# Asking for the tokens of a tile ahead of its first weights, with four buffers late in the expert loop of a fused transformer layer

## The chip, the cores and the metric

The kernel runs on one core of one Trainium2 chip. The metric is device time in microseconds (us) for one launch of the whole layer. TensorE (PE) does matrix products and transposes, VectorE (DVE) and ScalarE (ACT) the elementwise work, GpSimd (POOL) indirect transfers and some elementwise work, and SyncE (SP) issues plain DMA transfers. Each engine runs its own list of instructions in order. They meet only at semaphores: an instruction that waits holds up all that stands behind it on its engine.

## What is computed

```python
x = x + attn(layernorm(x))                # efficient attention, one head of 256
x = x + xattn(layernorm(x), ctx)          # causal cross attention, 16 heads of 64
y = layernorm(x)                          # 4096 tokens of 256
probs = softmax(y @ router_w + router_b)  # 16 experts
topw, topi = top_k(probs, 4); topw /= sum(topw)
for e in range(16):                       # each token counts for its 4 experts only
    x += (gelu(y @ w1[e] + b1[e]) @ w2[e] + b2[e]) * gate[:, e]
```

x is 8 batches (B) of 512 tokens by 256, w1 is 16 x 256 x 512, w2 is 16 x 512 x 256, all fp32. Every product is made of three products in a reduced fp32 form, from a high and a low part of each side (`split3`): a "split" of a matrix is one copy that rounds to the high part and one subtraction that gives the low part.

## The kernel before

Three stages follow each other: the first attention, the cross attention with the routing of each batch, and the expert tiles. The change lies in the last, and in the few microseconds where the second goes over into it.

**One list for all engines.** `attention_plan()` writes a list of (step, index) by hand. Each engine walks that one list and emits its own part of each step (the functions `tensor`, `scalar`, `vector`, `gpsimd`, `sync`), so the order of the list is the order of every engine's queue.

**Routing.** The rows of each batch, with their gates and token numbers, are scattered by POOL into `rows_dram`, sorted by expert (steps `scatter`, and `scatter_last` for the last batch). Rows that fill up an expert's last tile are written by SP (step `pad`, two experts in each of the iterations 9 to 16, two transfers per expert).

**Expert tiles.** 79 tiles (`MOE_TILES`) of 256 rows of one expert each. Which expert and which row a tile starts at is read from tables, for the first 24 tiles (`SURE_TILES`) from a table made before the last two batches were routed. The steps of tile j are:
- `load_x` (SP): 256 rows of 273 floats into `x_in[j % 2]`. It waits until tile j - 2 has been turned (`t_pe`) and its gates copied out (`tail_set`).
- `load_w1` (SP): the 512 KB of its expert's w1 into `w1_raw[j % 2]` (the tiles `ahead.ctx32` and `ahead.x1_0`, free by then). It waits until tile j - 2's w1 has been split (`w1_hi`, `w1_lo`).
- `turn_x`: four transposes (PE) into one bank, the high part by ACT, the low part (`x_lo`) and the copy of the gates (`tail`) by DVE.
- `split_w1` (DVE): the two parts of w1, and the tile's b1.
- `hidden`: 24 matmuls (PE), GELU and high part (ACT), low part (DVE).
- `results`: 24 matmuls with w2 (PE), scaling by the gate into `y` (ACT), and two indirect transfers that add the rows to `out` (POOL). POOL first waits until the adds of the one or two tiles before have landed, where these may touch the same tokens (at a change of expert), and ACT waits for the add of tile j - 3.

Iteration j of the loop holds, in this order: load x of j+2, turn x of j+1, hidden of j, split w1 of j+2, load w1 of j+4, results of j-1. The routing steps of the last batch (`CHAIN`) are strewn over the iterations 1 to 10. Up to tile 11 (`CHAIN_END`) all tiles use one bank for `turn_x`, since the other belongs to these steps.

**Between the stages** the 16 matrices of w2 are split (`high_w2` by ACT, `low_w2` by DVE, or by POOL for those in `LOW_BY_POOL`). The last seven of them stand around `turn_x` 0 and `output` of the last batch; `results` of any tile waits for all.

Of the kernel before, what the change touches and what calls it, by code (L numbers as in the profile page):

```python
# [930 lines left out]
def attention_plan():  # L931
    plan = [("begin", None), ("project_k", 0), ("project_v", (0, 0)), ("project_q", 0), ("project_v", (0, 1))]
    split_w2 = lambda *mine: [(step, e_) for step in ("high_w2", "low_w2") for e_ in mine]
    for n in range(B * PAIRS + 1):
# [60 lines left out]
def cross_attention(nc, sems, spent, d, x1_dram, x1_stored, out, rows_dram, routing, W, projecting, ahead, kept, hold, plan):  # L995

    with ExitStack() as stack:
# [118 lines left out]
        def sync(sp, w, step, at):  # L1116
# [7 lines left out]
            elif step == "add_b2" and at[1] == 1:  # L1124
                b = at[0]
                w.wait_ge(b2_ev, at)
# [511 lines left out]

def experts(nc, sems, d, rows_dram, out, routing, held, ahead, kept, gone):

    with ExitStack() as stack:
# [334 lines left out]
```

## Time and profile before

| | |
|---|---|
| time, median of 3 runs | 1805.8 us (1803.61 to 1812.94) |
| the profiled execution's own time | 1795.01 us |
| its span, first to last instruction | 1793.3 us |
| mean granted TensorE clock | 0.972 of full speed |
| busy: PE, DVE, ACT, POOL | 91%, 67%, 60%, 28% |

The span is cut below at starts of `turn_x`, the first step of a tile on PE. Each stretch then holds a whole number of tiles: tiles 0 to 3, 4 to 11, 12 to 19, 20 to 76, and the last two with the end. In the views `ex_X` is the bank of `turn_x`, `kept_x` is `x_in`, `ahead_ctx` and `ahead_x` are `w1_raw`, `ex_w` the split w1, `ex_H` and `ex_Y` the banks of `hidden` and `results`, `expert_rows<-ahead_spare` a `pad`, and `experts_w_hi`, `experts_w_lo` the two parts of w2. The granted clock is either full (2.4 GHz) or half (1.2 GHz); a mean between them says how the stretch was divided.

### The profile page before, as it was taken

What the parts mean: (1) busy time and instruction counts of PE and PEld (TensorE: products, weight loads), DVE (VectorE), ACT (ScalarE), POOL (GpSimd) and SP (SyncE); (2) the same over time, 40 slices, a digit from 0 to 9 for tenths busy, and PEclk for the clock granted to TensorE, in tenths of its full rate; (3) what the DMA queues carried; (4) which work ended last, traced back from release to release, by engine and by line L of the source; (5) the groups of instructions that cost most, each with busy time, mean ns of one, the idle gap of its engine ahead of it and who ended that gap; (6) DMA issues with size and microseconds to landing.
All of it is one profiled execution on the core that took longest, in us unless ns stands there. A gap on an engine that the chain in (4) does not pass through costs nothing.

```text
span 1793.3 us, 35763 instructions
## 1 busy us (share of the span) xinstructions
PE 1623.1 (91%) x12470; PEld 1360.6 (76%) x12470; DVE 1195.2 (67%) x2752; ACT 1078.5 (60%) x2702; POOL 505.0 (28%) x432
## 2 busy tenths in 40 slices
PE   5899889999999999999999999878778989888886
PEld 4788767777776777777777777578778888888886
DVE  6988756677677776777677766876445555555552
ACT  4555466766666666766676666856345555655553
POOL 2444300000302103012030130344544444443444
PEclk9999989999999999999999999989889999999998
DMA  3121110000201101001010021645766666665663
GB/s 93 36 83 71 46 50 1 1 24 1 86 1 44 44 1 63 24 20 68 1 57 30 7 80 46 210 124 134 206 177 141 153 148 145 156 147 132 154 153 62
DMA packets 94976, 144.54 MB, mean 81 GB/s; under 512 B 12576, under 2 KB 55120, under 8 KB 94800
## 3 DMA queue, kind: packets, MB, share of 16 engines
q1 hardware_dynamic: 64176, 101.40, 18.2%
q0 software_dynamic: 28896, 38.62, 11.4%
q8 instruction: 103, 1.69, 0.4%
q10 hardware_dynamic: 1728, 2.23, 0.4%
q14 instruction: 73, 0.60, 0.1%
HBM read 90.76 MB, written 51.46 MB: 79 GB/s over the span
## 4 chain that ended last, share of the span: by engine, by line
PE 38%; ACT 18%; DVE 13%; DMA 10%; issue 5%; SPq 3%; POOL 0%; POOLq 0%; DVEq 0%; ACTq 0%
DMA kept_x<-expert_rows 9%; PE ex_H L1750 7%; ACT xa_prob L1334 7%; PE xa_work L1174 5%; PE xa_work L1249 5%; PE xa_S L1203 4%; PE xa_work L1185 4%; PE xa_work L1232 4%; PE xa_work L1220 4%; ACT xa_probT L1348 3%; DVE xa_nmax L1452 3%; DVE ex_w L1821 2%; ACT ex_h L1785 2%; PE ex_X L1732 2%; DVE xa_prob L1464 2%
## 5 line engine op out<-in xcount | busy, mean ns | idle before, releaser
L1334 ACT ACTIVATE xa_prob<-xa_S,xa_nmax 128x512 f32<-128x512 f32 (+3 forms) x512 | 266.3, 535 | 131.2 <-DVE xa_nmax L1452 130.4
L1867 POOL DMA_INDIRECT out<-ex_y,ahead_bits x158 | 249.6, 1580 | 327.4 <-ACT ex_y L1798 193.2
L1750 PE MATMUL ex_H<-ex_xT,ex_w 128*128 128x256 f32 x1896 | 265.8, 300 | 0.0
L1750 PEld LDWEIGHTS ex_H<-ex_xT,ex_w 128*128 128x128 f32 x1896 | 251.7, 207 | 0.0
L1765 PE MATMUL ex_Y<-experts_w_hi,ex_hT 128*128 x1264 | 236.4, 280 | 0.0
L1838 DVE TENSOR_TENSOR ex_hT<-ex_h,ex_hT 128x512 fp32r<-128x512 f32 x158 | 109.4, 693 | 175.7 <-ACT ex_hT L1790 175.7
L1765 PEld LDWEIGHTS ex_Y<-experts_w_hi,ex_hT 128*128 128x128 f32 x1264 | 198.8, 188 | 0.0
L1452 DVE TENSOR_REDUCE xa_nmax<-xa_S 128x2 f32<-128x1024 f32 (+3 forms) x256 | 197.8, 814 | 1.2 <-PE xa_S L1208 1.2
L1625 POOL DMA_INDIRECT expert_rows<-kept_xn,kept_rows x112 | 110.9, 990 | 274.0 <-DVE xa_prob L1464 249.5
L1348 ACT ACTIVATE xa_probT<-xa_work 128x512 f32<-128x512 f32 x256 | 139.7, 602 | 77.3 <-PE xa_work L1220 77.3
L1765 PE MATMUL ex_Y<-experts_w_lo,ex_hT 128*128 x632 | 176.3, 279 | 0.0
L1464 DVE TENSOR_SCALAR xa_prob<-xa_prob,xa_sums 128x512 f32<-128x512 f32 (+3 forms) x512 | 169.4, 384 | 6.8
L1220 PE MATMUL xa_work<-ahead_ident,xa_prob 128*128 128x128 f32 x1280 | 160.0, 279 | 8.4 <-DVE xa_prob L1464 6.1
L1785 ACT ACTIVATE ex_h<-ex_H,kept_b 128x256 f32<-128x256 f32 x316 | 131.7, 468 | 58.5 <-PE ex_H L1750 50.8
L1798 ACT ACTIVATE ex_y<-ex_Y,ahead_bits 128x256 f32<-128x256 f32 x158 | 66.4, 471 | 160.5 <-PE ex_Y L1765 152.1
L1220 PEld LDWEIGHTS xa_work<-ahead_ident,xa_prob 128*128 128x128 f32 x1280 | 140.2, 142 | 19.6 <-DVE xa_prob L1464 9.0
L1232 PE MATMUL xa_work<-xa_probT,xa_v 128*64 128x512 f32 (+3 forms) x1024 | 154.1, 444 | 0.8 <-ACT xa_probT L1345 0.8
L1732 PE MATMUL ex_X<-ahead_ident,kept_x 128*128 128x128 f32 x316 | 53.1, 293 | 89.4 <-DMA kept_x<-expert_rows 81.1
L1232 PEld LDWEIGHTS xa_work<-xa_probT,xa_v 128*64 128x64 f32 x1024 | 68.4, 138 | 81.4 <-issue 67.6
L1459 DVE RECIPROCAL xa_sums<-xa_sums 128x2 f32<-128x2 f32 (+1 forms) x192 | 32.2, 168 | 144.0 <-ACT xa_prob L1334 144.0
L1765 PEld LDWEIGHTS ex_Y<-experts_w_lo,ex_hT 128*128 128x128 f32 x632 | 118.6, 188 | 0.0
L1732 PEld LDWEIGHTS ex_X<-ahead_ident,kept_x 128*128 128x128 f32 x316 | 36.0, 146 | 99.6 <-DMA kept_x<-expert_rows 91.3
(359 smaller groups left out, 3747.4 us busy)
## 6 DMA issues: line engine op xcount, KB each, us to landing
kept_x<-expert_rows SPq DMA_DIRECT2D x79, 273.0 KB, 4.5
ahead_ctx<-in_w SPq DMA_DIRECT2D x40, 512.0 KB, 3.7
ahead_x<-in_w SPq DMA_DIRECT2D x39, 512.0 KB, 3.7
experts_w_lo<-in_w SPq DMA_DIRECT2D x6, 1024.0 KB, 6.0
expert_rows<-ahead_spare SPq DMA_DIRECT2D x32, 136.5 KB, 3.8
a_x<-in_x SPq DMA_DIRECT2D x8, 512.0 KB, 4.6
x_rows<-a_x_both SPq DMA_DIRECT2D x8, 512.0 KB, 5.4
ahead_ctx<-in_ctxT SPq DMA_DIRECT2D x8, 512.0 KB, 4.4
```

The lines of the kernel that those rows point to most:

```text
L1220: m = pe.transpose(PJ[:, col:col + P], prob[n % 2][:, odd, PROB_AT[i] + j * P:PROB_AT[i] + (j + 1) * P], ident[:])
L1232: m = pe.matmul(OB[HD * odd:HD * odd + HD, j * P:512], v[n % 2][:, j, first_col + HD * odd:first_col + HD * odd + HD], probT[:, odd, PROB_ ...
L1334: m = act.activation(prob[n % 2][:, odd, PROB_AT[i]:PROB_AT[i] + width], SB[slot[at]][:, odd, col:col + width], ACT.Exp, bias=nmax[n % 2][ ...
L1348: act.activation(probT[:, odd, first_col:first_col + 512], bank(step, at)[:], ACT.Copy).then_inc(t_ev.of(at), 1)
L1452: m = dve.tensor_reduce(nmax[n % 2][:, i, :], SB[slot[at]][:, :, SCORE_COL[i]:SCORE_COL[i] + (i + 1) * P], AX.X, ALU.max, negate=True)
L1464: m = dve.tensor_scalar(part, part, sums[n % 2][:, i, odd:odd + 1], None, ALU.mult)
L1625: pool.indirect_dma_start(rows_dram, bass.IndirectOffsetOnAxis(rows_i[b % 2][:, t, k:k + 1], 0), xn3[:, t, :], None).then_inc(scattered[of ...
L1732: m = pe.transpose(x_bank(j)[:, c * ROWS + a * P:c * ROWS + (a + 1) * P], x_in[j % NX][:, a, c * P:(c + 1) * P], ident[:])
L1750: m = pe.matmul(bank[:, (f % 2) * ROWS:(f % 2 + 1) * ROWS], ww[:, c, f * P:(f + 1) * P], xx[:, c, :], start=(i == 0), stop=(i == len(terms ...
L1765: m = pe.matmul(bank[:, a * D:(a + 1) * D], hh[:, f, a * P:(a + 1) * P], W2[:, bass.ds(own * WE + f * D, D)], start=(i == 0), stop=(i == l ...
L1785: i = act.activation(h32[:, f, :], HB[2 * (j % 2) + u][:, (f % 2) * ROWS:(f % 2 + 1) * ROWS], ACT.Gelu, bias=b1[j % 2][:, f:f + 1])
L1867: pool.indirect_dma_start(out, bass.IndirectOffsetOnAxis(tail[j % NT][:, a, 0:1].bitcast(I32), 0), y[j % NY][:, a, :], None, compute_op=AL ...
```

## The change

It has four parts. (1) In each iteration the load of x is now that of tile j+3, and it stands behind `turn_x` of j+1: on SP, x of a tile now precedes w1 of the tile behind it, where before w1 of tile j+4 stood ahead of x of tile j+3. (2) Tiles from 20 on use four buffers for x and for raw w1; the new ones for x lie in `xn3`, those for w1 in the room that the tile `x2` leaves. (3) Tiles 0, 1 and 2 turn their x in two banks by turns. (4) Around the first tiles the last seven splits of w2, four scatters and the stores of `x2` stand elsewhere, and POOL makes the low part of three matrices instead of two.

```diff
-TURN_AT, LOW_BY_POOL = 14, (10, 13)
+TURN_AT, LOW_BY_POOL = 14, (10, 13, 11)
...
-    plan += [*(("scatter", (b - 1, i, end, 1)) for i, _ in SCATTER_AT[1]), ("add_b2", (b - 1, 1)),
-             ("split_w1", 0), ("turn_x", 0), ("warm", None), *split_w2(8, 0), ("output", (b, 1, 0)),
-             ("output", (b, 1, 1)), ("load_w1", 2), ("split_w1", 1), *split_w2(10, 9, 13, 12, 11), ("load_w1", 3)]
+    plan += [("add_b2", (b - 1, 1)), ("store_x2", b - 1), ("split_w1", 0), ("turn_x", 0), ("load_x", 2), ("warm", None), *split_w2(10, 8, 13, 11),
+             *(("scatter", (b - 1, i, end, 1)) for i, _ in SCATTER_AT[1]), ("output", (b, 1, 0)), ("output", (b, 1, 1)),
+             ("load_w1", 2), ("split_w1", 1), ("load_w1", 3), *high_w2(0)]
     for j in range(MOE_TILES + 1):
         chain = CHAIN.get(j, [])
-        steps = [("load_x", j + 2), ("turn_x", j + 1), ("turn_tables", None), ("hidden", j), *chain[:1], ("split_w1", j + 2),
-                 ("load_w1", j + 4), ("results", j - 1), *chain[1:]]
+        steps = [("turn_x", j + 1), ("load_x", j + 3), ("turn_tables", None), *(high_w2(9, 12) + low_w2(0) if j == 0 else []),
+                 ("hidden", j), *(low_w2(9, 12) if j == 0 else []), *chain[:1], ("split_w1", j + 2), ("load_w1", j + 4), ("results", j - 1), *chain[1:]]
...
-                 TURN_AT: [("give_tables", None)]}.get(j, [])
+                 11: [("store_x2", B - 1)], TURN_AT: [("give_tables", None)]}.get(j, [])
...
-NX, NW = 2, 2
-CHAIN_END = 12
+FEW, MORE, MORE_AT = 2, 4, 20
+CHAIN_AT, CHAIN_END = 3, 12
...
+        buffer_of = {j: j % (FEW if j < MORE_AT else MORE) for j in tiles}
+        in_buffer_before = {j: max((i for i in tiles[:j] if buffer_of[i] == buffer_of[j]), default=None) for j in tiles}
...
-        bank_of = {j: 0 if j < CHAIN_END else j % 2 for j in tiles}
+        bank_of = {j: 0 if CHAIN_AT <= j < CHAIN_END else j % 2 for j in tiles}
...
-                w.wait_ge(scattered, last, j >= SURE_TILES)
+                w.wait_ge(scattered, last, j >= SURE_TILES or buffer_of[j] >= FEW)
...
-                w.wait_ge(t_pe, j - NX, j >= NX)
-                w.wait_ge(tail_set, j - NX, j >= NX)
+                before = in_buffer_before[j]
+                w.wait_ge(t_pe, before, before is not None)
+                w.wait_ge(tail_set, before, before is not None)
...
-                w.wait_ge(w1_hi, j - NW, j >= NW)
-                w.wait_ge(w1_lo, j - NW, j >= NW)
+                before = in_buffer_before[j]
+                w.wait_ge(w1_hi, before, before is not None)
+                w.wait_ge(w1_lo, before, before is not None)
+                w.wait_ge(gone["x2_out"], B - 1, j >= MORE_AT)
...
-                w.wait_ge(gone["low_w2"], 11)
-                w.wait_ge(gone["low_w2_pool"], 13)
+                w.wait_ge(gone["low_w2"], 12)
+                w.wait_ge(gone["low_w2_pool"], 11)
```

SP's queue at the head of the loop, before the change: x of tile 2 (`kept_x0`), raw w1 of tile 4 (`ahead_ctx32`), x of tile 3 (`kept_x1`). The TENSOR_LOAD and ISA rows read the tile's expert or first row.

```order
L1696 TENSOR_LOAD routing_first_row
L1696 ISA x2
L1697 ISA
L1697 DMA kept_x0<-expert_rows 128x546
L1713 TENSOR_LOAD routing_owner
L1713 ISA x2
L1714 ISA
L1714 DMA ahead_ctx32<-in_w1 128x2x512
L1696 TENSOR_LOAD routing_first_row
L1696 ISA x2
L1697 ISA
L1697 DMA kept_x1<-expert_rows 128x546
```

The same place now: x of tile 3, raw w1 of tile 4, x of tile 4. (x of tile 2 has moved up ahead of raw w1 of tile 2.)

```order
L1701 TENSOR_LOAD routing_first_row
L1701 ISA x2
L1702 ISA
L1702 DMA kept_x1<-expert_rows 128x546
L1720 TENSOR_LOAD routing_owner
L1720 ISA x2
L1721 ISA
L1721 DMA ahead_ctx32<-in_w1 128x2x512
L1701 TENSOR_LOAD routing_first_row
L1701 ISA x2
L1702 ISA
L1702 DMA kept_x0<-expert_rows 128x546
```

The load of x of each tile has moved ahead of the w1 load that stood in front of it, and this holds for every tile up to the last.

DVE around the split of w1 of tile 1 (`ex_w_10`, `ex_w_11`), before: three low parts of w2 stand between it and the gates and `x_lo` of tile 1 (`ahead_bits`, `ex_xT`).

```order
L1819 CAST ex_w_10<-ahead_x_0 128x1024
L1821 TENSOR_TENSOR ex_w_11<-ahead_x_0,ex_w_10 128x1024
L1825 TENSOR_LOAD routing_owner
L1825 ISA x2
L1826 ISA
L1826 COPY kept_b_1<-ahead_bits 128x4
L1549 TENSOR_TENSOR experts_w_lo<-experts_w_lo,experts_w_hi 128x1024 x3
L1830 COPY ahead_bits<-kept_x 128x34
L1832 TENSOR_TENSOR ex_xT<-ex_X,ex_xT 128x512
L1838 TENSOR_TENSOR ex_hT<-ex_h,ex_hT 128x512 x2
```

And now:

```order
L1826 CAST ex_w_10<-ahead_x_0 128x1024
L1828 TENSOR_TENSOR ex_w_11<-ahead_x_0,ex_w_10 128x1024
L1832 TENSOR_LOAD routing_owner
L1832 ISA x2
L1833 ISA
L1833 COPY kept_b_1<-ahead_bits 128x4
L1837 COPY ahead_bits<-kept_x 128x34
L1839 TENSOR_TENSOR ex_xT<-ex_X,ex_xT 128x512
L1550 TENSOR_TENSOR experts_w_lo<-experts_w_lo,experts_w_hi 128x1024
L1845 TENSOR_TENSOR ex_hT<-ex_h,ex_hT 128x512 x2
L1550 TENSOR_TENSOR experts_w_lo<-experts_w_lo,experts_w_hi 128x1024 x2
```

The three low parts now stand behind `x_lo` of tile 1, one of them ahead of the low parts of `hidden` of tile 0 and two behind.

POOL at the same place, before: all sixteen scatters of batch 6, then two low parts, then the norm of batch 7 and the adds of tile 0.

```order
L1614 IOTA kept_xn 128x4
L1625 DMA expert_rows<-kept_xn,kept_rows 69632x273 x16
L1604 TENSOR_TENSOR experts_w_lo<-experts_w_lo,experts_w_hi 128x1024 x2
L1599 TENSOR_TENSOR xa_ln_rstd<-xa_ln_rstd,ahead_power 128x4
L1867 DMA out<-ex_y,ahead_bits 4352x256 x2
```

And now:

```order
L1615 IOTA kept_xn 128x4
L1626 DMA expert_rows<-kept_xn,kept_rows 69632x273 x12
L1605 TENSOR_TENSOR experts_w_lo<-experts_w_lo,experts_w_hi 128x1024 x3
L1626 DMA expert_rows<-kept_xn,kept_rows 69632x273 x4
L1600 TENSOR_TENSOR xa_ln_rstd<-xa_ln_rstd,ahead_power 128x4
L1874 DMA out<-ex_y,ahead_bits 4352x256 x2
```

Three low parts now stand ahead of the last four scatters.

## Rows read from the trace of the kernel before

**Rows 1.** Stretches: us; busy (x instructions) of PE, PEld, DVE, ACT, POOL; clock; DMA share; GB/s.

```profile
1158.70:1195.90 37.20, 25.19 (x186) 24.40 (x184) 32.57 (x52) 20.98 (x36) 18.65 (x12) 0.86 0.42 127
1195.90:1262.60 66.70, 55.48 (x463) 54.62 (x463) 40.93 (x114) 37.90 (x79) 32.62 (x26) 0.97 0.62 152
1262.60:1341.40 78.80, 60.63 (x421) 59.72 (x421) 35.23 (x70) 34.02 (x72) 35.05 (x27) 0.83 0.71 183
1341.40:1756.20 414.80, 366.00 (x2964) 357.97 (x2964) 233.38 (x398) 238.99 (x511) 179.99 (x114) 0.98 0.64 148
1756.20:1793.30 37.10, 21.03 (x176) 20.83 (x176) 8.39 (x15) 13.57 (x30) 15.94 (x10) 0.83 0.34 40
```

**Rows 2.** The same view, transposes of `turn_x` alone (PE, PEld), two stretches.

```profile
1262.60:1341.40 78.80, 6.86 (x33) 4.70 (x33) 0.83 0.71 183
1341.40:1756.20 414.80, 37.00 (x228) 24.81 (x228) 0.98 0.64 148
```

**Rows 3.** Waits, whole span: us in total, times, longest us.

```profile
PE ex_X L1732 <- DMA kept_x<-expert_rows: 81.1, 46, 5.7
POOL out L1867 <- POOLq L1863: 61.5, 17, 4.8
```

**Rows 4.** Chain that ended last, around tiles 33 to 35: start us, us, what.

```profile
1436.31 2.89 PE ex_H L1750 x24
...
1442.09 1.24 DVE ex_w L1821
...
1444.13 0.38 SPq L1714
...
1445.33 3.65 DMA kept_x<-expert_rows
1449.03 0.66 PE ex_X L1732 x4
```

**Rows 5.** Timeline of PE: turns of tiles 39 and 40.

```profile
1477.88 0.66 PE L1732 MATMUL ex_X<-ahead_ident,kept_x 128*128 128x128 f32 x4 [1.95 <-DMA kept_x<-expert_rows]
...
1484.08 0.60 PE L1732 MATMUL ex_X<-ahead_ident,kept_x 128*128 128x128 f32 x4
```

**Rows 6.** The chain again, at tile 12.

```profile
1253.23 0.37 SPq L1714
...
1258.70 3.83 DMA kept_x<-expert_rows
...
1263.69 5.11 PE ex_H L1750 x24
```

**Rows 7.** DMA issues, 1262 to 1324 us: KB each, median us to landing.

```profile
out<-ex_y,ahead_bits POOLq DMA_INDIRECT x13, 6.0
```

**Rows 8.** DMA issues, 1400 to 1750 us.

```profile
kept_x<-expert_rows SPq DMA_DIRECT2D x48, 273.0 KB, 4.5
ahead_ctx<-in_w SPq DMA_DIRECT2D x24, 512.0 KB, 3.6
...
out<-ex_y,ahead_bits POOLq DMA_INDIRECT x96, 4.7
```

**Rows 9.** Timelines of DVE, POOL, ACT and PE around tile 1.

```profile
1168.82 2.33 DVE L1826 COPY kept_b<-ahead_bits 128x4 f32 x1
1171.06 5.62 DVE L1549 TENSOR_TENSOR experts_w_lo<-experts_w_lo,experts_w_hi 128x1024 fp32r<-128x1024 f32 x3
...
1168.49 5.98 POOL L1604 TENSOR_TENSOR experts_w_lo<-experts_w_lo,experts_w_hi 128x1024 fp32r<-128x1024 f32 x2
...
1161.40 6.74 ACT L1384 ACTIVATE experts_w_hi<-experts_w_lo 128x1024 fp32r<-128x1024 f32 x7
...
1177.52 1.09 PE L1732 MATMUL ex_X<-ahead_ident,kept_x 128*128 128x128 f32 x4 [8.03 <-DVE ex_xT L1832]
```

**Rows 10.** Timeline of POOL: the first add of tiles 77 and 78.

```profile
1778.63 1.54 POOL L1867 DMA_INDIRECT out<-ex_y,ahead_bits  x1 [3.36 <-POOLq L1863]
...
1785.05 1.54 POOL L1867 DMA_INDIRECT out<-ex_y,ahead_bits  x1 [3.03 <-POOLq L1863]
```

More of the change, by code:

```diff
@@ L959, in attention_plan @@
         if done >= 1 and p == 0:
-            first.append(("add_b2", (done - 1, 1)))
+            first += [("add_b2", (done - 1, 1)), ("store_x2", done - 1)]
         if coming < B:
@@ L1123, in sync @@
                 sp.dma_start(ctx32[:], d['ctxT'][b].rearrange("(k p) s -> p k s", p=P)).then_inc(ctx_in.of(b), 16)
[L1124 to L1126 removed]
+            elif step == "store_x2":
+                b = at
+                w.wait_ge(b2_ev, (b, 1))
                 sp.dma_start(out[b * S:(b + 1) * S, :].rearrange("(t p) c -> p t c", p=P), x2[:]
@@ L1645, in experts @@
         ident, rows_i, xn3, pads = ahead.ident, kept.rows_i[(B - 1) % 2], kept.xn3, ahead.spare
-        b1T, tail, x_in, sent = kept.b1T, kept.tail, kept.x_in, gone["scattered"]
+        b1T, tail, sent = kept.b1T, kept.tail, gone["scattered"]
         as_w1 = lambda tile: tile[:].rearrange("p a b -> p (a b)").rearrange("p (k n) -> p k n", k=KC)
-        w1_raw = [as_w1(tile) for tile in (ahead.ctx32, ahead.x1_0)]
         two = lambda name, shape: tuple(sb(f"{name}{part}", shape, F32R) for part in range(2))
@@ L1656, in experts @@
         tables, pad_i = Tables(sb, kept.scr), sb("pad_i", [1, E], I32)
-        sb("room_of_x2_and_gates", [P, LATE_ROOM])
+        sb("room_of_gates", [P, LATE_ROOM])
+        w1_raw = [*(as_w1(tile) for tile in (ahead.ctx32, ahead.x1_0)), *(sb(f"w1_raw{i}", [P, KC, FF])[:] for i in (2, 3))]
+        x_in = [*kept.x_in, *(xn3[:].rearrange("p (i a) c -> p i a c", a=RT)[:, i] for i in range(2))]
         w1, xT = [w1_of(0), w1_1], [xT_of(0), xT1]
@@ L1671, in experts @@
         scattered = landed("scattered", [(t, k) for t in range(N_TILES) for k in range(TOPK)])
-        x_loaded = [landed(f"x_loaded{i}", tiles[i::NX]) for i in range(NX)]
+        x_loaded = [landed(f"x_loaded{i}", [j for j in tiles if buffer_of[j] == i]) for i in range(MORE)]
         added = [sent[i].go_on([(j, a) for j in tiles[i::NY] for a in range(RT)]) for i in range(NY)]
@@ L1676, in experts @@
         w1_hi, w1_lo, b1_ev = (signal(n, tiles) for n in ("w1_hi", "w1_lo", "b1_ev"))
-        w1_loaded = [landed(f"w1_loaded{i}", tiles[i::NW]) for i in range(NW)]
+        w1_loaded = [landed(f"w1_loaded{i}", [j for j in tiles if buffer_of[j] == i]) for i in range(MORE)]
         h_pe, gelu, h_hi, h_lo = (signal(n, halves) for n in ("h_pe", "gelu", "h_hi", "h_lo"))
         y_pe, y_ev = signal("y_pe", tiles), signal("y_ev", tiles)
-        bank_of = {j: 0 if j < CHAIN_END else j % 2 for j in tiles}
+        bank_of = {j: 0 if CHAIN_AT <= j < CHAIN_END else j % 2 for j in tiles}
         x_bank = lambda j: XB[bank_of[j]]
```

29 lines of the change are left out of this document (15 added, 14 removed).

## The prediction

> **What bounds the kernel now.** I read the stretches first [rows 1]. From the first turn on, the expert part takes 634.6 us (37.2 + 66.7 + 78.8 + 414.8 + 37.1) of the 1793.3. PE is busiest in all but the first of them and yet idles: 48.8 us of 414.8 in the long one, 18.2 of 78.8 in the third. The waits say for what [rows 3]: 46 times for x of a tile, 81.1 us in all. DVE, ACT and POOL are far from full, and the DMA engines are at 0.64 in the long stretch.
>
> The chain of what ended last shows why x is late [rows 4]. It goes round once in two tiles: `hidden` of tile 33 starts at 1436.31; GELU and its parts follow; DVE ends the split of w1 of tile 34 at 1443.3; only then may SP ask for raw w1 of tile 36 (1444.13), and 1.20 us later, behind it in the same queue, for x of tile 35 (1445.33). That lands after 3.65 us, and the turn of tile 35 begins at 1449.03. The turn of tile 33 had freed the buffer of tile 35 at about 1437, so SP holds that request back some 8 us for a wait that belongs to another transfer.
>
> What a tile costs without the wait stands in the timeline of PE [rows 5]: from the turn of tile 39 to that of tile 40, 6.20 us. 13 tiles of the long stretch show 6.19 to 6.25. It holds 57 tiles (228 transposes [rows 2]), so 7.28 us each; the floor is 57 x 6.20 = 353.4 us, and 61.4 us lie above it.
>
> **The change, stretch by stretch.** *Tiles 20 to 76.* The request for x of tile j+3 now waits for the turn of tile j+1 and for nothing of w1 of j+4. Take tile 35: its request would stand at 1438 (turn of 33, plus SP's 1.2 us), land with the median 4.5 us [rows 8] at 1442.5, and be needed at 1435.7 + 2 x 6.20 = 1448.1: 5.6 us to spare. With four buffers more is to spare. Raw w1 is then next in line: asked for at 1444.13, landed 3.6 us later at 1447.7, needed by DVE at about 1441.4 + 12.4 = 1453.8. If it now queues behind x, it is late by at most one x, 4.5 us, and still in time. So PE's own 6.20 us is next, and the 61.4 us can go. Two things are taken off. At the end each tile's add waits until the one before has landed: 6.42 us from the first add of tile 77 to that of 78 [rows 10], over PE's 6.20; I give six such gaps up to 0.6 us each, 3.6 us (bounds 0 and 6). For odd waits that come back I choose 3 us (bounds 0 and 20: the DMA share rises from 0.64 to 0.64 x 7.28 / 6.20 = 0.75, and the third stretch, at 0.71, is the nearest row with longer landings). Term: -55 us.
>
> *Tiles 12 to 19* (33 transposes [rows 2], one of them a neighbour's) take 78.8 us, 9.85 each. Here SP also issues four pad transfers between raw w1 and x [rows 6]: 1253.23 to 1258.70 is 5.47 us where it was 1.20, and PE, after the long idle, runs at half clock: 5.11 us for the 24 matmuls of `hidden` that take 2.89 [rows 4], granted clock 0.83 [rows 1]. In the new order the pads still stand ahead of a load of x, but of one that is due a whole tile later. Three floors: PE 8 x 6.20 = 49.6 us; SP 8 x (5.47 + 1.20) = 53.4; DMA engines 0.71 x 78.8 = 55.9. The highest is DMA, which never packs without gaps; I take 60, a term of -19 us (bounds -8, if x still comes late half of the time, and -29, the floor of PE).
>
> *Tiles 4 to 11* take 66.7 us, in which PE works 55.5, routing of the last batch included. The 11.2 us of idle are nearly all waits for x. I leave 1.2 us: -10 us (bounds -6 and -11).
>
> *Tiles 0 to 3* take 37.2 us, 12.0 of them idle on PE. The longest wait of PE, 8.03 us, is for `x_lo` of tile 1 [rows 9]: DVE first copied b1 (2.33 us for four columns) and made three low parts of w2 (5.62). Those three now stand behind it, and the turn of tile 2 has a bank of its own; `hidden` of tile 1 still needs `x_lo`. ACT does five high parts ahead of the turn of tile 1 instead of seven, 2 x 0.96 us less (seven take 6.74 [rows 9]), no longer on the path. Against it: POOL now makes three low parts at this place, and its two held DVE up. A subtraction of that shape takes 1.24 us alone [rows 4], so the three lost 5.62 - 3.72 = 1.9 us and the copy some 2.2: 4.1 us for two low parts on POOL, 6.1 for three. So 5.62 - 2.0 = 3.6 us are sure, and the whole idle, 12, is the other end; what goes besides is the wait for x of tile 4 and half clock after the idle. I take -8 us. The four scatters that move behind POOL's splits (POOL was then idle until the norm of batch 7) and the later store of `x2` are hidden: SP and POOL have idle time there, and the store lands nine tiles ahead of the first load that waits for it, tile 20's w1 asked in iteration 16. Without that cover it would cost one landing, some 4 us (512 KB land in 3.6 [rows 8]).
>
> For this stall the Trainium skill has a rule against the change (SBUF — State Buffer, section Who interferes with whom): a DVE instruction with two SBUF inputs and a GpSimd one that reads SBUF exclude each other for the whole instruction. By it three low parts on POOL, 5.98 / 2 = 3.0 us each [rows 9], could hold DVE for 9.0 us instead of 6.1, and this term would be -5 instead of -8. The trace agrees that such a lock exists (2.33 us for a copy of four columns), not on how much of it falls on the path.
>
> **Sum.** -55 - 19 - 10 - 8 = -92 us. Against the profiled execution's own 1795.0 us that is 1703. The median of the runs shown, 1805.8, lies 10.8 higher, so I expect a median near **1713 us**.
>
> **The rivals.** (a) *The wait for x is only partly removed.* At 0.75 busy DMA engines, with adds on the same engines, x and w1 land late in places, and an idle PE then falls to half clock again. For it: landings of adds rise from 4.7 [rows 8] to 6.0 us [rows 7] in the densest stretch. Against: x has 5.6 us to spare, more than any such rise. At half of each term the gain is 46: 1760 us. (b) *It goes better:* no DMA floor in tiles 12 to 19 (-29), no loss at the end and no odd waits (-61), -11, -12: 113 us, 1693. (c) *It does nothing:* the new wait (turn and gate copy of j+1) might be as late as the old one. That needs the turn of j+1 to lie after the split of w1 of j+2, and in the chain [rows 4] it lies 7 us before: 1806. (d) *Slower,* by the adds. POOL starts a tile's add at a change of expert only when the last has landed; two issues and a landing make 6.42 us at 4.7 us landing. If every tile had to wait so, and landing rose to 6.6 with the denser traffic, a tile would take 8.3 us, 79 of them 657 against 634.6 now: +22, 1828. It decides from a landing of 6.3 us on (634.6 / 79 = 8.03). Against it: POOL has waited so only 17 times, 61.5 us [rows 3], and the others absorb it, since ACT waits only for the add three tiles back.
>
> **How the numbers follow.** Chances: forecast 0.65 (its own range 1697 to 1732, from the bounds of the four terms taken together), a 0.20, b 0.08, c 0.03, d 0.04. Within 0.5%, about 9 us, a measurement of this kernel can't tell a change; all of the forecast, a and b lie below that: faster 0.93, same 0.03, slower 0.04. The range reaches from b's 1693 to a's 1760.
>
> **What would show it.** Right: the wait of PE for x falls from 81.1 us to under 15; tile to tile 6.2 to 6.3 us from tile 20 on; granted clock near 1.00 in the long stretch and over 0.9 in the third; that stretch near 60 us with a DMA share over 0.9; the chain no longer passes through the split of w1; the wait for `x_lo` of tile 1 shrinks to 2 to 5 us. Wrong: PE waiting for `ex_w` (w1 late), landings of x above 8 us, POOL's waits above 100 us with ACT waiting for adds, or half clock without idle before it.

## The result and the profile after

The changed kernel takes 1700.9 us (median of 4 runs, 1697.6 to 1709.1) against 1807.3 us for the kernel before in the same comparison (1803.6 to 1812.9): a ratio of 0.942, 95% interval 0.937 to 0.946, faster by 106 us. Its profiled execution took 1697.64 us with a span of 1695.9 us.

The stretches of the profile after, cut at the same turns as [rows 1]: us; busy (x instructions) of PE, PEld, DVE, ACT, POOL; clock; DMA share; GB/s.

```profile
1165.00:1194.80 29.80, 23.83 (x186) 23.21 (x185) 28.43 (x45) 20.23 (x34) 20.34 (x13) 0.94 0.46 135
1194.80:1249.20 54.40, 53.31 (x465) 53.09 (x465) 40.69 (x107) 37.49 (x80) 33.10 (x24) 1.00 0.73 179
1249.20:1306.10 56.90, 50.30 (x420) 49.41 (x420) 37.59 (x81) 33.91 (x74) 38.36 (x29) 1.00 1.02 264
1306.10:1657.80 351.70, 350.12 (x2965) 349.91 (x2966) 231.97 (x399) 232.98 (x513) 193.07 (x116) 1.00 0.75 176
1657.80:1695.90 38.10, 20.94 (x178) 20.73 (x176) 9.46 (x16) 13.53 (x30) 15.81 (x11) 0.83 0.33 39
```

Against [rows 1] the five stretches change by -7.4, -12.3, -21.9, -63.1 and +1.0 us, together -103.7. The first turn starts 6.3 us later (1165.0 after 1158.7), so the span loses 97.4. In the long stretch PE is now busy 350.1 of 351.7 us: nothing but its own work is left. Of the 63.1 us there, 47.2 are idle time that has gone (48.8 before, 1.6 now) and 15.9 are busy time (366.0 to 350.1, the clock 1.00 where it was 0.98). In tiles 12 to 19 the busy time fell by 10.3 us of the 21.9, the clock from 0.83 to 1.00. So a part of the gain is the clock, which PE is granted in full once it no longer idles. (The DMA share adds up the time that packets took, and can pass 1.00.)

The waits of the whole span, us in total, times, longest us, beside [rows 3]:

```profile
POOL out L1874 <- POOLq L1870: 82.2, 24, 5.9
DVE ahead_bits L1837 <- DMA out<-ex_y,ahead_bits: 19.9, 13, 5.4
DVE xa_nmax L1453 <- remote: 7.4, 6, 1.3
...
PE ex_H L1757 <- DVE ex_xT L1839: 5.2, 2, 3.6
PE ex_X L1739 <- DMA kept_x<-expert_rows: 4.6, 3, 1.9
```

PE's wait for x has gone from 81.1 us in 46 pieces to 4.6 in 3. What has grown is POOL's wait for the landing of earlier adds (61.5 to 82.2), and from it comes the second row: DVE may copy the gates of a tile only when the add of five tiles back has landed, since there are five buffers for them.

The timeline of PE, two turns of the long stretch, beside [rows 5], and that of tile 34:

```profile
1367.55 0.60 PE L1739 MATMUL ex_X<-ahead_ident,kept_xn 128*128 128x128 f32 x4
1373.69 0.60 PE L1739 MATMUL ex_X<-ahead_ident,kept_xn 128*128 128x128 f32 x4
...
1392.09 0.60 PE L1739 MATMUL ex_X<-ahead_ident,kept_xn 128*128 128x128 f32 x4
```

6.14 us from the first to the second, with no bracket behind the row, so no wait.

The timeline of SP (when a DMA is issued) at the same place shows the new order at work:

```profile
1369.81 0.38 SPq L1721 DMA_DIRECT2D ex_w_raw<-in_w  x1
1371.02 0.33 SPq L1702 DMA_DIRECT2D kept_xn<-expert_rows  x1
1376.17 0.38 SPq L1721 DMA_DIRECT2D ex_w_raw<-in_w  x1
1377.70 0.34 SPq L1702 DMA_DIRECT2D kept_xn<-expert_rows  x1
```

One raw w1 and one x per tile as before. The x asked for at 1371.02 is that of tile 34, which PE turns at 1392.09 (last row of the fence before): 21 us ahead. Before the change x of tile 35 was asked for 3.7 us ahead of its turn [rows 4]. Each x still has a w1 in front of it, but there is time enough to wait for it. PE never waits for `ex_w`, so w1 isn't late either.

### The profile page after: what moved, and what is told of

Its sections match the earlier page's. It is cut to its first block, busy times and chain, and to the rows that moved or that the text cites. A ratio compares the mean times of both kernels' runs of the same rounds, so it can differ in the third digit from the quotient of the medians.

```text
span 1695.9 us, 35759 instructions
## 1 busy us (share of the span) xinstructions
PE 1592.5 (94%) x12470; PEld 1338.2 (79%) x12470; DVE 1192.4 (70%) x2751; ACT 1071.8 (63%) x2702; POOL 523.8 (31%) x433
## 4 chain that ended last, share of the span: by engine, by line
PE 51%; ACT 16%; DVE 10%; issue 4%; DMA 3%; SPq 1%; POOL 1%; POOLq 0%; another core or an unknown queue 0%; DVEq 0%; ACTq 0%
PE ex_H L1757 10%; PE ex_Y L1772 10%; ACT xa_prob L1335 8%; PE xa_work L1250 5%; PE xa_work L1175 5%; PE xa_S L1204 4%; PE xa_work L1186 4%; PE xa_work L1233 4%; PE xa_work L1221 4%; ACT xa_probT L1349 4%; DVE xa_nmax L1453 3%; DMA out<-ex_y,ahead_bits 3%; DVE xa_prob L1465 2%; PE ex_X L1739 2%; DVE xa_q1lo L1446 1%
## 5 line engine op out<-in xcount | busy, mean ns | idle before, releaser
L1874 POOL DMA_INDIRECT out<-ex_y,ahead_bits x158 | 263.8, 1670 | 212.0 <-POOLq L1870 82.2
L1757 PE MATMUL ex_H<-ex_xT,ex_w 128*128 128x256 f32 x1896 | 247.4, 287 | 5.2 <-DVE ex_xT L1839 5.2
L1757 PEld LDWEIGHTS ex_H<-ex_xT,ex_w 128*128 128x128 f32 x1896 | 233.1, 192 | 5.6 <-issue 5.6
L1792 ACT ACTIVATE ex_h<-ex_H,kept_b 128x256 f32<-128x256 f32 x316 | 132.0, 471 | 12.7 <-PE ex_H L1757 11.7
L1233 PEld LDWEIGHTS xa_work<-xa_probT,xa_v 128*64 128x64 f32 x1024 | 68.3, 137 | 81.1 <-issue 67.3
L1335 ACT ACTIVATION_READ_ACCUMULATOR xa_prob<-xa_S,xa_nmax 128x1 f32 x512 | 108.2, 211 | 0.0
L1797 ACT ACTIVATE ex_hT<-ex_h 128x512 fp32r<-128x512 f32 x158 | 100.1, 634 | 5.0
```

The source lines that it names most:

```text
L1233: m = pe.matmul(OB[HD * odd:HD * odd + HD, j * P:512], v[n % 2][:, j, first_col + HD * odd:first_col + HD * odd + HD], probT[:, odd, PROB_ ...
L1335: m = act.activation(prob[n % 2][:, odd, PROB_AT[i]:PROB_AT[i] + width], SB[slot[at]][:, odd, col:col + width], ACT.Exp, bias=nmax[n % 2][ ...
L1757: m = pe.matmul(bank[:, (f % 2) * ROWS:(f % 2 + 1) * ROWS], ww[:, c, f * P:(f + 1) * P], xx[:, c, :], start=(i == 0), stop=(i == len(terms ...
L1792: i = act.activation(h32[:, f, :], HB[2 * (j % 2) + u][:, (f % 2) * ROWS:(f % 2 + 1) * ROWS], ACT.Gelu, bias=b1[j % 2][:, f:f + 1])
L1874: pool.indirect_dma_start(out, bass.IndirectOffsetOnAxis(tail[j % NT][:, a, 0:1].bitcast(I32), 0), y[j % NY][:, a, :], None, compute_op=AL ...
```

## The experiments

Theory: SP's queue was the loop. x stood behind a request that waited for the split of w1 two tiles back, and the new order alone breaks that. Rivals: the four buffers do it (the split waited for is then four tiles back); or the new start has a large share. All times are medians; a ratio is to the kernel before, run in turn with it on the same chip, with its 95% interval.

### Each part alone

In the first four runs the kernel before took 1800.5 us.

**order_only**, part (1) on the kernel before:

```diff
-             ("split_w1", 0), ("turn_x", 0), ("warm", None), *split_w2(8, 0), ("output", (b, 1, 0)),
+             ("split_w1", 0), ("turn_x", 0), ("load_x", 2), ("warm", None), *split_w2(8, 0), ("output", (b, 1, 0)),
...
-        steps = [("load_x", j + 2), ("turn_x", j + 1), ("turn_tables", None), ("hidden", j), *chain[:1], ("split_w1", j + 2),
+        steps = [("turn_x", j + 1), ("load_x", j + 3), ("turn_tables", None), ("hidden", j), *chain[:1], ("split_w1", j + 2),
```

> The kernel before with part (1) alone: x of tile j+3 asked for behind the turn of j+1. Theory: it brings the gains of all stretches but the first, 97 less 7 for tiles 0 to 3, so some 90 us: 1716 us, ratio 0.945 to 0.955. Rival (buffers needed too): the stretch of tiles 20 to 76 keeps half of its excess, 1745 us, ratio 0.965. Second rival: the order does nothing without the buffers, 1800 us.

Measured: 1692.1 us (1691.2 to 1695.3), ratio 0.9397 [0.9382, 0.9413], 108 us less than before. Its stretches:

```profile
1158.70:1192.50 33.80, 24.94 (x187) 24.56 (x186) 29.54 (x46) 19.95 (x34) 17.90 (x12) 0.85 0.41 120
1192.50:1245.70 53.20, 53.20 (x464) 53.07 (x463) 40.43 (x107) 37.09 (x79) 30.78 (x23) 1.00 0.73 177
1245.70:1303.10 57.40, 50.48 (x422) 49.46 (x421) 37.53 (x82) 33.95 (x74) 39.52 (x29) 1.00 1.04 273
1303.10:1655.20 352.10, 350.12 (x2964) 349.91 (x2965) 232.23 (x398) 232.80 (x512) 192.43 (x116) 1.00 0.76 175
```

All but the first are those of the changed kernel within 1.2 us, and the first too loses 3.4 of its 37.2 us. Both rivals are out: with two buffers and the old start the whole of the long stretch's gain is there. It gained 108 us where I had written 90: the 97 I started from held the 6.3 us lost ahead of the first turn, which this run doesn't lose (last section), and the 7 taken off for the first stretch should have been 4. The 9 that remain lie between profiled executions and medians: the profile before (1795.0) is 5.5 us below the median before in this comparison, and this run's profiled execution (1695.3) is 3.2 above its own. From span to span the gain is 99.8 us.

**two_buffers**, the changed kernel without part (2):

```diff
-FEW, MORE, MORE_AT = 2, 4, 20
+FEW, MORE, MORE_AT = 2, 4, 79
```

> The changed kernel with two buffers of x and of raw w1 for all tiles. Theory (the order of SP's requests alone breaks the loop): x of a tile may be asked for as soon as its buffer was turned, 5.6 us ahead of need with the 4.5 us landing taken off, and raw w1 has 6 us; so nothing changes, 1701 us, at most 6 more, ratio to the kernel before 0.939 to 0.946, and the period from tile 20 on stays 6.13 to 6.2 us. Rival (the four buffers carry the long stretch): with two, PE waits again in part of the 57 tiles; half of the 63 us that the stretch gained come back, 1730 us or more, ratio 0.957 or more.

Measured: 1693.3 us (1690.8 to 1701.4), ratio 0.9421 [0.9394, 0.9448]. Its long stretch:

```profile
1299.60:1649.60 350.00, 349.97 (x2965) 349.98 (x2966) 234.22 (x399) 233.55 (x513) 192.33 (x115) 1.00 0.75 177
```

PE is busy all of 57 tiles of 6.14 us. In the new order two buffers are enough. (The changed kernel itself did not run in this comparison; its ratios of 0.942 and 0.940 elsewhere say the same.)

**buffers_only**, part (2) alone:

```diff
-        steps = [("turn_x", j + 1), ("load_x", j + 3), ("turn_tables", None), *(high_w2(9, 12) + low_w2(0) if j == 0 else []),
-                 ("hidden", j), *(low_w2(9, 12) if j == 0 else []), *chain[:1], ("split_w1", j + 2), ("load_w1", j + 4), ("results", j - 1), *chain[1:]]
+        steps = [("load_x", j + 2), ("turn_x", j + 1), ("turn_tables", None), ("hidden", j), *chain[:1], ("split_w1", j + 2),
+                 ("load_w1", j + 4), ("results", j - 1), *chain[1:]]
```

(and the start of before, with its bank for the first tiles; the stores of `x2` stay where the changed kernel has them, since the new buffers need their room).

> The order and the start of the kernel before, with four buffers of x and raw w1 from tile 20 on. Theory: the loop of before went through the buffer of raw w1 (the request waited for the split two tiles back); with four buffers that split is four tiles back, so the loop is broken from tile 20 on as well, and only tiles 20 to 76 gain: 61 of the 63 us, 1745 us, ratio 0.963 to 0.972, tiles 4 to 19 as before. Rival (the order in the queue is what counts, whatever the buffers): x still stands behind raw w1 and the long stretch stays at 7.3 us per tile, 1800 us, ratio 0.995 or more.

Measured: 1731.8 us (1728.3 to 1737.0), ratio 0.9613 [0.9596, 0.9630], 69 us less than before (58 from span to span; 61 were expected). Tiles 12 to 19, and 20 to 76:

```profile
1265.90:1346.40 80.50, 59.30 (x421) 58.39 (x421) 35.00 (x70) 33.89 (x72) 34.90 (x27) 0.83 0.68 184
1346.40:1697.80 351.40, 350.05 (x2964) 349.84 (x2965) 231.90 (x397) 232.12 (x511) 185.04 (x114) 1.00 0.75 175
```

Tiles 12 to 19 stay near [rows 1] (80.5 us for 78.8), tiles 4 to 11 too (69.0 for 66.7), and from tile 20 on nothing is left to gain. So either part breaks the loop by itself: the order (for all tiles) by taking x out from behind the wait, the buffers (only where there is room for them) by making the wait end two tiles earlier. In the changed kernel the second adds nothing to the first.

**start_only**, parts (3) and (4) alone (x of tile 2 keeps its early place ahead of w1 of tile 2):

```diff
-        steps = [("turn_x", j + 1), ("load_x", j + 3), ("turn_tables", None), *(high_w2(9, 12) + low_w2(0) if j == 0 else []),
+        steps = [*([("load_x", j + 2)] if j else []), ("turn_x", j + 1), ("turn_tables", None), *(high_w2(9, 12) + low_w2(0) if j == 0 else []),
...
-FEW, MORE, MORE_AT = 2, 4, 20
+FEW, MORE, MORE_AT = 2, 4, 79
```

> The old order of loads in the loop and two buffers, with parts (3) and (4), the new start. Theory: only the stretch of tiles 0 to 3 gains, 7 us: 1800 us, ratio 0.993 to 0.998. Rival: the gain of the first tiles hangs on x being there in time as well, and the wait goes over to tile 4: 1807 us, ratio 1.000. If the six waits of 1.2 us for another core or an unknown queue, once per batch of the cross attention, belong to the new program, the time before the first turn is 1165 us here too and the total is up to 1807 us; if they belong to the execution, 1158 to 1160.

Measured: 1800.0 us (10 runs, 1785.5 to 1801.5), ratio 0.9986 [0.9958, 1.0015]: no difference clear of noise.

```profile
1154.60:1189.00 34.40, 26.54 (x186) 25.72 (x185) 28.92 (x46) 20.23 (x34) 21.32 (x13) 0.85 0.47 138
1189.00:1258.70 69.70, 57.28 (x465) 56.19 (x463) 43.76 (x119) 38.76 (x81) 33.13 (x26) 0.94 0.57 141
```

The first stretch gains 2.8 us and the second loses 3.0. That fits the rival: what is saved ahead of a loop that waits for x is given back at the next wait for x. It isn't shown. buffers_only, with the old start, also has 69.0 us in the second stretch where the kernel before has 66.7, so 2 to 3 us there come without the new start, and a gain of 2.8 us in the whole would lie inside the interval.

### The start on top of the order

Four variants of the changed kernel in one comparison, the kernel before at 1797.9 us.

**start_undone**: the `plan`, the `steps` for tile 0, `LOW_BY_POOL` and `CHAIN_AT` of before, with the new order, the new places of the stores of `x2`, and four buffers:

```diff
-TURN_AT, LOW_BY_POOL = 14, (10, 13, 11)
+TURN_AT, LOW_BY_POOL = 14, (10, 13)
...
-        steps = [("turn_x", j + 1), ("load_x", j + 3), ("turn_tables", None), *(high_w2(9, 12) + low_w2(0) if j == 0 else []),
-                 ("hidden", j), *(low_w2(9, 12) if j == 0 else []), *chain[:1], ("split_w1", j + 2), ("load_w1", j + 4), ("results", j - 1), *chain[1:]]
+        steps = [("turn_x", j + 1), ("load_x", j + 3), ("turn_tables", None), ("hidden", j), *chain[:1], ("split_w1", j + 2),
+                 ("load_w1", j + 4), ("results", j - 1), *chain[1:]]
```

> The changed kernel with the start of before (parts 3 and 4 undone, LOW_BY_POOL of two), order of loads and four buffers kept. Theory: tiles 0 to 3 go back to some 37 us, so 7 us more than the changed kernel: 1708 us, ratio to before 0.944 to 0.948. Rival (x in time was what the first tiles lacked as well): 1702 us. The six waits of 1.2 us in the cross attention: present if they belong to the changed program's later part, absent if to the start.

Measured: 1694.7 us (1692.7 to 1695.7), ratio 0.9429 [0.9407, 0.9451].

**one_bank**, part (3) undone:

```diff
-CHAIN_AT, CHAIN_END = 3, 12
+CHAIN_AT, CHAIN_END = 0, 12
```

> The changed kernel with part (3) undone: one bank for the turns of tiles 0 to 11. Theory: the turn of tile 2 then waits for x_lo of tile 1, and the turn of tile 1 for that of tile 0; PE has hidden of tile 0 and output of batch 7 to do in between, so the loss is 1 to 3 us: 1702 to 1704 us. Rival (the two banks are what the 7 us of the first tiles came from): 1708 us.

Measured: 1689.9 us (1687.2 to 1690.5), ratio 0.9400 [0.9377, 0.9422]; no loss against pool_two or pads_first below, which have the second bank, so theory and rival both missed: no worth of the second bank can be seen.

**pool_two**, matrix 11 back to DVE:

```diff
-TURN_AT, LOW_BY_POOL = 14, (10, 13, 11)
+TURN_AT, LOW_BY_POOL = 14, (10, 13)
```

> The changed kernel with the low part of w2's matrix 11 made by DVE again, two low parts on POOL. Theory (POOL's low parts hold DVE up by about as much as DVE saves): the same within 2 us, 1700 to 1703. Rival (the rule that a subtraction of DVE and one of POOL exclude each other for the whole instruction, with 3.0 us each): the third costs DVE 3 us against the 1.24 it saves, so two on POOL is 2 us faster if that place is on the path.

Measured: 1691.2 us (6 runs, 1688.6 to 1705.5), ratio 0.9412 [0.9388, 0.9436]. Its profiled execution is the slowest, 14 us above the median. The first stretch of start_undone, of one_bank and of pool_two, one row each:

```profile
1162.90:1194.30 31.40, 24.30 (x186) 23.85 (x185) 27.69 (x45) 19.77 (x34) 14.75 (x10) 0.88 0.39 120
```

```profile
1157.40:1186.90 29.50, 23.70 (x186) 23.11 (x185) 28.61 (x45) 20.04 (x34) 20.72 (x13) 0.94 0.47 137
```

```profile
1163.80:1193.90 30.10, 25.59 (x187) 24.86 (x186) 28.14 (x46) 19.66 (x34) 16.27 (x10) 0.87 0.43 129
```

The second bank and the third low part on POOL change nothing that can be seen (29.8 with both). So the step from 31.4 or 33.8 (order_only) to about 30, 2 to 4 us, is left to the new places of the other splits and of the four scatters; no run parts these two. Start_undone is 3.5 to 4.8 us above the medians of the other three variants here, every run of it above every run of one_bank.

**pads_first**, each iteration's pads ahead of its raw w1:

```diff
-                 ("hidden", j), *(low_w2(9, 12) if j == 0 else []), *chain[:1], ("split_w1", j + 2), ("load_w1", j + 4), ("results", j - 1), *chain[1:]]
+                 ("hidden", j), *(low_w2(9, 12) if j == 0 else []), *chain[:1], ("split_w1", j + 2), *(("pad", e_) for e_ in (2 * (j - 9), 2 * (j - 9) + 1) if 0 <= e_ < E), ("load_w1", j + 4), ("results", j - 1), *chain[1:]]
...
-        plan += [("pad", e_) for e_ in (2 * (j - 9), 2 * (j - 9) + 1) if 0 <= e_ < E]
```

> The changed kernel with each iteration's four pad transfers issued ahead of that iteration's load of raw w1 instead of behind results. Theory of SP (the waits for x at tiles 14, 15 and 20 come from SP being busy with pads after it has waited for the split): they vanish, 3 to 5 us less: 1697 us, ratio to before 0.936 to 0.941, tiles 12 to 19 in 52 to 54 us. Rival (the DMA engines, whose share was 1.02 in that stretch, set it): no change there, 56 to 57 us and 1701 us.

Measured: 1691.1 us (1688.5 to 1694.3), ratio 0.9416 [0.9394, 0.9439]. Tiles 12 to 19 take 57.0 us at a DMA share of 1.05, and PE still waits for x, 3.7 us in one piece. SP's theory falls, though it is not yet shown that the DMA engines are the limit.

### What is left in tiles 12 to 19, and the start once more

Four in one comparison, the kernel before at 1813.9 us.

**changed_again** and **order_again** are the changed kernel and order_only once more, with no edit.

> The changed kernel once more, beside the one that has only the new order of loads. Theory (that the start and the four buffers give next to nothing on top of the order): the two ratios lie within 0.003 of each other. Rival (the new start's 4.3 us, which the stretch of tiles 0 to 3 showed, arrive): the changed kernel is 4 us ahead, 0.0025. The six waits of 1.2 us in the cross attention, if they belong to the changed program, are here again and the first turn starts at 1165 us; if to one execution, it starts at 1155 to 1163.

> The kernel before with the new order of loads alone, once more, as the partner of the changed kernel: ratio to the kernel before 0.940 to 0.943.

Measured: 1704.3 us (1703.2 to 1709.8), ratio 0.9395 [0.9361, 0.9430], and 1708.0 us (1706.2 to 1710.3), ratio 0.9411 [0.9377, 0.9445]. The changed kernel is 3.8 us ahead, and the ratios lie within 0.003 of each other, so this alone can't part theory and rival. The profiles can, for one execution each. Tiles 0 to 3 and 12 to 19 of the changed kernel, then of order_only:

```profile
1169.40:1198.70 29.30, 24.78 (x186) 24.17 (x185) 28.14 (x45) 19.94 (x34) 18.80 (x11) 0.88 0.44 133
1253.16:1313.99 60.83, 53.35 (x420) 52.47 (x420) 36.30 (x81) 34.04 (x73) 36.68 (x28) 0.94 0.96 248
```

```profile
1174.10:1209.30 35.20, 25.69 (x187) 24.72 (x186) 28.15 (x46) 20.29 (x34) 16.24 (x12) 0.85 0.37 115
1263.71:1319.28 55.57, 50.57 (x421) 49.49 (x421) 35.34 (x79) 33.20 (x73) 39.94 (x28) 1.00 1.02 271
```

The new start gains 5.9 us in the first stretch, tiles 12 to 19 take 5.3 more, and from the first turn to the end the changed kernel is 1.1 us slower; its lead in span, 3.7 us, lies ahead of the first turn (1169.4 against 1174.1). So the start's gain is not shown to arrive here. Two_buffers (1693.3, new start) and order_only (1692.1, old start) show none either, while start_undone loses 3.5 to 4.8. Over the three comparisons the new start is worth -1 to 5 us, 0.3% at most.

**pads_joined**, the two pad transfers of an expert as one:

```diff
-                for a in range(RT):
-                    sp.dma_start(rows_dram[bass.ds(row, ROWS), :].rearrange("(p a) c -> p a c", p=P)[:, a, :],
-                                 pads[:, a * PAD_STEP:a * PAD_STEP + PAY]).then_inc(padded.of((j, a)), 16)
+                both = bass.AP(tensor=pads, offset=pads[:].offset, ap=[[PAY + (RT - 1) * PAD_STEP, P], [PAD_STEP, RT], [1, PAY]])
+                sp.dma_start(rows_dram[bass.ds(row, ROWS), :].rearrange("(p a) c -> p a c", p=P), both).then_inc(padded.of((j, 0)), 16)
```

> The changed kernel with the two pad transfers of an expert made one: half of SP's issues, the same bytes. Theory (the DMA engines, at a share of 1.02, set what is left in tiles 12 to 19): the stretch stays at 56 to 58 us and PE still waits for x there. Rival (SP, whose pads take 2.6 to 5.5 us per tile, is late with x): the waits for x at tiles 14, 15 and 20 go, 52 to 54 us, total 3 to 5 us less.

Measured: 1706.6 us (1705.8 to 1707.5), ratio 0.9404 [0.9370, 0.9438]: half of the issues, nothing gained. Tiles 12 to 19 take 60.0 us, more than the 56 to 58 expected, but as long as in the changed kernel beside it (60.8).

**pads_joined_double**, the same and once more the same bytes to a place that nothing reads:

```diff
+                sp.dma_start(aside[j], both).then_inc(padded.of((j, 1)), 16)
```

> The changed kernel with each expert's pads as one transfer, and a second transfer of the same bytes to a place that nothing reads: SP issues as many transfers as in the changed kernel, and 546 KB more per iteration move in iterations 9 to 16. Theory (DMA engines are the limit there): at the stretch's 264 GB/s that is 2.1 us per tile, five such tiles in the stretch, so tiles 12 to 19 take 65 to 69 us and the total is 8 to 12 us more, 1706 us with the changed kernel at 1696. Rival (SP's issues are the limit): no change, 57 us.

Measured: 1725.3 us (1723.3 to 1730.5), ratio 0.9513 [0.9478, 0.9549], 18.7 us above pads_joined. Tiles 4 to 11 and 12 to 19 of pads_joined, then of pads_joined_double:

```profile
1202.00:1256.40 54.40, 53.30 (x465) 53.08 (x463) 40.55 (x107) 37.57 (x80) 32.36 (x24) 1.00 0.73 178
1256.40:1316.40 60.00, 53.32 (x421) 52.42 (x421) 36.01 (x80) 33.74 (x72) 37.84 (x28) 0.94 1.00 251
```

```profile
1199.60:1254.00 54.40, 53.24 (x464) 53.01 (x463) 40.48 (x107) 37.65 (x80) 33.22 (x24) 1.00 0.73 178
1254.00:1332.60 78.60, 59.62 (x420) 58.35 (x421) 36.56 (x80) 34.27 (x72) 41.08 (x30) 0.85 1.11 258
```

With SP issuing as often as in the changed kernel, 16 more transfers of 273 KB (4.5 MB) lengthen the stretch by 18.6 us: 4.5 MB at 258 GB/s are 17.3. The bytes that the DMA engines move are the limit there, not the number of issues. I had counted only the five iterations that lie in the stretch; but the tiles before it show none of the extra bytes (54.4 us and 178 GB/s in both), and SP's timeline has the sixteen transfers from 1251.25 to 1320.15 us, so all eight iterations' land in this stretch, and 8 to 12 should have been 17. On PE the 18.6 us are 12.4 more of waits for x (17.0 for 4.6) and 6.3 more of busy time at a clock of 0.85. Two things stay open. Every pad goes through the same queue as x, so no run parts full engines from x standing behind the pads in its own queue. And with the same bytes the stretch varies: 56.9 and 60.8 us in the two profiles of the changed kernel, at 264 and 248 GB/s.

## Why the prediction was right

- **What bounds the kernel.** Right: the wait of x behind raw w1 in SP's queue. Shown by order_only, which moves nothing else.
- **Tiles 20 to 76, -55 us.** The stretch changed by -63.1. The step "the floor is 57 x 6.20 = 353.4 us" was mis-sized: with no waits the period is 6.14 us, and two_buffers takes 350.0 for 57 tiles, 3.4 less. All 13 periods of 6.19 to 6.25 in the profile before begin with a turn that had waited, and that turn takes 0.66 us for 0.60 [rows 5]. The 3 us for odd waits became 1.7 (351.7 - 350.0). The 3.6 us for serialized adds at the end of the span belongs to the last stretch, which grew by 1.0; the adds do run some 6.5 us apart there. Together the three make the 8.3 us (3.4 + 1.3 + 3.6) by which this term was too small.
- **What the four buffers are for.** The text rested the gain on the order, with 5.6 us to spare for two buffers. That was right, and two_buffers shows it. That the buffers alone would do as much was not said; buffers_only shows it.
- **Tiles 12 to 19, -19 us to 60.** Measured 56.9, and 55.6 to 60.8 over the other runs with the new order and the same bytes. The floor named, DMA engines at 55.9, is the one that ends the gain, as far as the runs part it: share 1.02, no effect of SP's issues (pads_first, pads_joined), full effect of bytes (pads_joined_double). "Never packs without gaps" had no row behind it, and the shares of 1.00 to 1.05 here speak against it. As a margin it was too careful by some 3 us in this run and right in others. Beside PE's own 50.3 us, what is left is 4.6 of waits for x (the last of them, 1.1, at the turn of tile 20) and 2.0 for the table of tiles.
- **Tiles 4 to 11, -10 us.** -12.3, and -13.5 in order_only, where PE is busy 53.20 of 53.20 us. The term had left out the clock: with the idle went the half clock (0.97 to 1.00), and PE's work fell from 55.5 us to 53.3 (53.2 in order_only). The 1.2 us of idle allowed for is there in the changed kernel's profile (54.4 less 53.3) and not in order_only's; it is a part of what the last section tells.
- **Tiles 0 to 3, -8 us.** The size was right (-7.4), the working not. 3.4 us come from the order (order_only), which this term held only as "the wait for x of tile 4": PE waited 2.7 us for it before, and 0.5 for x of tile 3, and waits for neither now. "The turn of tile 2 has a bank of its own" is worth nothing (one_bank). The 4.1 us for two low parts on POOL hold for the kernel before [rows 9]; "6.1 for three" was too much, as the timelines of POOL and DVE after show:

```profile
1169.23 8.10 POOL L1605 TENSOR_TENSOR experts_w_lo<-experts_w_lo,experts_w_hi 128x1024 fp32r<-128x1024 f32 x3 [1.13 <-ACT experts_w_hi L1385]
```

```profile
1169.58 2.08 DVE L1833 COPY kept_b<-ahead_bits 128x4 f32 x1 [0.34 <-issue]
...
1172.27 2.83 DVE L1550 TENSOR_TENSOR experts_w_lo<-experts_w_lo,experts_w_hi 128x1024 fp32r<-128x1024 f32 x1
1175.02 1.28 DVE L1475 TENSOR_TENSOR xa_x<-xa_work,xa_x 128x512 f32<-128x512 f32 x2
1176.21 1.68 DVE L1826 CAST ex_w<-ahead_x 128x1024 fp32r<-128x1024 f32 x1
...
1179.07 0.19 DVE L1833 COPY kept_b<-ahead_bits 128x4 f32 x1
...
1182.19 2.35 DVE L1550 TENSOR_TENSOR experts_w_lo<-experts_w_lo,experts_w_hi 128x1024 fp32r<-128x1024 f32 x2
...
1190.21 0.69 DVE L1826 CAST ex_w<-ahead_x 128x1024 fp32r<-128x1024 f32 x1
```

Beside POOL's 8.10 us the copy takes 2.08 for 0.19, a subtraction 2.83 for 1.2, and the rounding copy 1.68 for about 0.7 (0.69 in the last row): 4.5 us for three low parts. In pool_two two of them hold up DVE by some 3.5 us; its timeline of DVE at that place has:

```profile
1168.97 5.96 DVE L1550 TENSOR_TENSOR experts_w_lo<-experts_w_lo,experts_w_hi 128x1024 fp32r<-128x1024 f32 x2 [0.60 <-ACT experts_w_hi L1385]
```

So, from one execution of each, the third costs about 1.0 and saves one subtraction of 1.2, and `x_lo` of tile 1 starts 14.3 and 14.2 us after the first turn. That the wait for it shrinks to 2 to 5 us was right: 3.6 us, the longest of the row of `ex_H` above. The two additions from `xa_work`, which is a PSUM bank, are not held up: 1.28 us, 0.64 each.

The Trainium skill (SBUF — State Buffer, section Who interferes with whom) names this pattern: a DVE instruction with two SBUF inputs contends with a GpSimd one that reads SBUF, and copies and casts can contend in the modes in which they use both ports, while a DVE instruction with at most one SBUF input outside such modes does not. The trace agrees on which instructions are held up, but for the small copy of the gates, which took its usual 0.17 us in that time, right behind the copy of b1. The 9 us that I had worked out from it as what DVE could lose was an upper bound, the whole overlap; the loss was 4.5, since DVE spent the rest of it on work that isn't held.

- **The sum and the median.** The stretches gave 103.7 us where 92 were forecast; 6.3 were lost again ahead of the first turn (below). "The median lies 10.8 higher" than the profiled execution was not a constant: the profile before came from an execution faster than all four timed beside the result, and after, the median lies only 3.3 higher. So the median came out 12 us under the forecast, 5.4 of them in the span (11.7 more gained, 6.3 lost) and the rest by this offset. That it lies inside the forecast's own range of 1697 to 1732 is in part luck: without the 6.3 us, which have nothing to do with the change, it would have been 1694.6, near the 1693 of rival (b).
- **Rivals.** (a) fell: x has slack enough at a DMA share of 0.75. (b) came true in two of its terms (-63.1 for its -61, -12.3 for its -11) and not in the others (-21.9 for -29, -7.4 for -12). (c) fell with the 4.6 us of waits. (d) exists in small: once the copy of the gates waits for an add, `x_lo` behind it is late, and from the turn of tile 38 to that of 39 it takes 7.93 us instead of 6.14. The timelines of PE, DVE and POOL after:

```profile
1416.64 0.60 PE L1739 MATMUL ex_X<-ahead_ident,kept_xn 128*128 128x128 f32 x4
...
1424.57 0.60 PE L1739 MATMUL ex_X<-ahead_ident,kept_xn 128*128 128x128 f32 x4
```

```profile
1417.76 0.19 DVE L1837 COPY ahead_bits<-kept_x 128x34 f32<-128x34 f32 x1 [5.38 <-DMA out<-ex_y,ahead_bits]
```

```profile
1402.13 2.02 POOL L1874 DMA_INDIRECT out<-ex_y,ahead_bits  x1 [3.60 <-POOLq L1870]
1404.45 1.59 POOL L1874 DMA_INDIRECT out<-ex_y,ahead_bits  x1 [0.30 <-issue]
1409.03 2.10 POOL L1874 DMA_INDIRECT out<-ex_y,ahead_bits  x1 [2.99 <-POOLq L1870]
1411.43 2.30 POOL L1874 DMA_INDIRECT out<-ex_y,ahead_bits  x1 [0.30 <-issue]
```

Twice in a row POOL waits for a landing before it may add, the adds fall 6.9 us apart, and the second landing comes at 1417.7, 6.3 us after its issue. A tile so delayed came once in the profiled run, at the same tile in most others, and not at all in two_buffers, pads_first, pads_joined and order_again: worth 1.7 us of the long stretch. The slow profiled execution of pool_two has two of them in a row, 8.30 and 11.04 us, and 356.9 us in the long stretch; there the copy of the gates waited 6.08 and 5.40 us for an add. The price at which (d) decides needs it at every tile.

## What to carry to other kernels

In a queue that one engine issues in order, a request with a wait holds up every request behind it: look in the chain for a transfer that was issued late although its own buffer had long been free, and put the request that is due first, and waits least, in front. More buffers cure the same stall by another way and only where there is room; try each alone before paying for both. A gain ahead of a loop that waits for something else may be given back at the loop's next wait, so measure such parts on top of the fix too, not only by themselves. And where an engine idles between its pieces of work, look at its granted clock: here 15.9 of the 63.1 us in the long stretch were busy time that became shorter.

## What the runs showed of the hardware

The 6.3 us ahead of the first turn are not the change. In the profiled run DVE waits six times, once for each of six batches of the cross attention, 1.2 to 1.3 us for what the profile can only call "remote", 7.4 us in all, and PE's own waits for the softmax there rise from 3.3 us to 9.4. The same wait in order_again, which has the instructions of before up to there:

```profile
DVE xa_nmax L1452 <- remote: 8.0, 6, 1.4
```

It is in all four profiled runs of the last comparison and in none of the eight of the other two, with the new start or the old; where it is, the first turn starts at 1165.0 to 1174.1 us, elsewhere (before included) at 1154.6 to 1163.8, and the median of the kernel before was 1813.9 in that comparison against 1800.5 and 1797.9. In the same five profiled runs, and in no other with the new order, PE also stands still for 1.1 us ahead of the turn of tile 12. The first comparison of experiments and the last ran on the same chip, one without it and one with it. So it belongs to the time of the runs, not to the kernel and not to the chip. What it is stays open. It is a reason to compare kernels within one comparison only: absolute medians of the same kernel moved by up to 16 us, more than parts (2) to (4) together.
